# A two-layer graph attention kernel: float8 masks, a check on VectorE, all layer-two comparisons on ScalarE, and a last run closed in halves

## The reference

```python
def layer0(h):                                   # 4 heads of 32 features
    Wh = (h @ W).reshape(N, 4, 32)
    e = leaky_relu(s_src[:, None, :] + s_dst[None, :, :], 0.2)
    attention = softmax(where(adj[:, :, None] > 0, e, -9e15), axis=1)
    return elu(einsum('ijh,jhd->ihd', attention, Wh).reshape(N, 128))

def layer1(x):                                   # hyperbolic, one head of 128 features
    x_tan = arctanh(|x|) * x / |x|
    e = leaky_relu(x_tan @ a[:128] + (x_tan @ a[128:]).T, 0.2)
    attention = softmax(where(adj > 0, e, -9e15), axis=1)
    return proj(expmap0(attention @ x_tan))

x = layernorm(x + layer0(x))
x = layernorm(x + layer1(x))
```

## Time and profile before

| what | us |
|---|---|
| median of 3 runs (lowest 977.76, highest 983.52) | 979.15 |
| the profiled execution, its own time | 978.17 |
| span of that execution in the trace | 976.3 |
| PE busy in the span | 854.6 |
| DVE busy | 771.7 |
| ACT busy | 759.4 |

### The profile page before, as it was taken

The page is one execution under the profiler, slowest core; times in us unless marked ns, Lnnn a source line. Parts: engine busy times, 40 slices in busy tenths (PEclk is TensorE's granted clock), DMA queues, the critical chain, the costliest instruction groups (busy, mean ns, idle before and its releaser), DMA issues.

```text
span 976.3 us, 24788 instructions
## 1 busy us (share of the span) xinstructions
PE 854.6 (88%) x10868; PEld 698.6 (72%) x10868; DVE 771.7 (79%) x1415; ACT 759.4 (78%) x933; POOL 94.9 (10%) x177
## 2 busy tenths in 40 slices
PE   8468999989999899999999992999999999899940
PEld 6468999989999899999998951555555555455520
DVE  3857898899988999889977897986859594949316
ACT  3868988888999879999889865367877686868751
POOL 2200000000000000000000100003131222212210
PEclk9879999999999999999999997899999999999975
DMA  8988278704568045040300040209494949576750
GB/s 143 172 83 203 64 71 95 222 24 49 66 75 228 24 39 73 25 196 23 110 3 24 19 177 1 98 12 361 170 388 152 402 152 368 190 308 220 279 211 12
DMA packets 55731, 135.01 MB, mean 138 GB/s; under 512 B 7746, under 2 KB 32708, under 8 KB 54980
## 3 DMA queue, kind: packets, MB, share of 16 engines
q0 software_dynamic: 26240, 83.90, 36.8%
q1 hardware_dynamic: 29380, 49.50, 13.9%
HBM read 162.60 MB, written 21.12 MB: 188 GB/s over the span
## 4 chain that ended last, share of the span: by engine, by line
PE 42%; DVE 26%; DMA 13%; ACT 11%; issue 7%; SPq 0%; DVEq 0%; ACTq 0%
PE bank L613 32%; DMA ring<-in_adj_dram 5%; PE bank L985 4%; ACT masks L695 4%; DMA moving<-in_adj_dram 4%; DVE ring L561 4%; DMA s_rows<-score_rows 3%; DVE ring L580 3%; ACT ring L548 2%; PE bank L464 2%; ACT s_rows L750 2%; ACT masks L451 2%; DVE ring L590 1%; PE bank L972 1%; DVE ring L584 1%
## 5 line engine op out<-in xcount | busy, mean ns | idle before, releaser
L613 PE MATMUL bank<-moving,ring 128*128 128x99 bf16 (+1 forms) x6400 | 461.8, 220 | 10.7 <-DVE ring L590 7.6
L613 PEld LDWEIGHTS bank<-moving,ring 128*128 128x128 fp8e4 x6400 | 390.9, 98 | 15.2 <-DVE ring L590 8.6
L548 ACT ACTIVATE ring<-s_rows,scores 128x1024 fp8e4<-128x1024 f32 x356 | 377.5, 1142 | 15.6 <-PE bank L613 14.2
L613 PE MATMUL bank<-moving,masks 128*128 128x99 bf16 x1792 | 243.3, 210 | 26.5 <-DVE ring L580 15.6
L613 PEld LDWEIGHTS bank<-moving,masks 128*128 128x128 fp8e4 x1792 | 176.7, 99 | 28.3 <-DVE ring L580 16.5
L985 PE MATMUL bank<-moving,masks 128*128 128x387 bf16 x1152 | 195.6, 328 | 0.0
L985 PEld LDWEIGHTS bank<-moving,masks 128*128 128x128 fp8e4 x1152 | 112.7, 98 | 79.1
L580 DVE SCALAR_TENSOR_TENSOR ring<-ring,masks 128x1024 int32<-128x1024 int32 x89 | 108.3, 1217 | 4.7 <-ACT ring L548 4.6
L590 DVE TENSOR_TENSOR ring<-masks,ring 128x1024 int32<-128x1024 int32 x72 | 88.2, 1225 | 26.4 <-PE bank L613 24.6
L750 ACT ACTIVATE s_rows<-moving,minus_one 128x1024 fp8e4<-128x1024 int32 x76 | 86.9, 1144 | 26.9 <-DMA moving<-in_adj_dram 26.3
L561 DVE TENSOR_SCALAR ring<-s_rows,neg_d 128x1024 uint8<-128x1024 f32 x156 | 106.9, 750 | 0.0
(11 more groups left out here) (183 smaller groups left out, 750.6 us busy)
## 6 DMA issues: line engine op xcount, KB each, us to landing
moving<-in_adj_dram POOLq DMA_DIRECT2D x76, 512.0 KB, 6.6
ring<-in_adj_dram POOLq DMA_DIRECT2D x52, 512.0 KB, 6.3
masks_kept<-masks SPq DMA_DIRECT2D x4, 4096.0 KB, 18.4
masks<-masks_kept SPq DMA_DIRECT2D x8, 2048.0 KB, 23.7
adj_tiles<-in_adj_dram POOLq DMA_DIRECT2D x24, 512.0 KB, 8.4
s_rows<-score_rows SPq DMA_DIRECT2D x14, 512.0 KB, 5.7
adj_tiles<-in_adj_dram POOLq DMA_DIRECT2D x16, 256.0 KB, 15.1
feat<-in_x_dram SPq DMA_DIRECT2D x4, 512.0 KB, 5.7
```

The lines of the kernel that those rows point to most:

```text
L548: last = act.activation(j_tile(below, k), s_rows[:, h % 2, :], ACT.Sign, bias=scores[:, g * JU + k, h:h + 1], saturate=False)
L613: last = pe.matmul(bank[b][:, at + lo:at + hi], mask, moving[:, j, h, lo:hi], start=first, stop=(j == T - 1), skip_group_check=True)
```

## The change

- **Float8 cast.** The transfers that load `adj` convert int32 to float8 (1 becomes 0x38) where they converted to uint8. ACT's copies out of PSUM scale by 8/7 where they scaled by 64, so a 1 is 0x40 again.
- **OR check of kept masks.** The check reads the 16 MB of `masks_kept`, in 32 parts of 512 KB, by POOL's queue. It runs on DVE: each part is combined with `seen` by a bitwise OR of 128 x 1024 int32. There are two buffers for loads, so part k is loaded when part k - 2 has been combined. The parts stand in DVE's list behind the splits of iteration e = 2, 3, 4, 5 and behind the closing of e = 6, in batches of 6, 6, 7, 6 and 7. `raise_flag` folds `seen` by four ORs and one AND. ACT does no checks.
- **All layer-two comparisons on ScalarE.** `signs` does eight tiles of each group in every run, and `split_group` is one AND with shift and one XOR on 128 x 1024 int32.
- **Two pairs of side buffers** at the change of layers: groups 1 and 3 use one, group 2 the other. Steps of groups 1 and 2 and the first pieces of the closing are written in another order on DVE and ACT.
- **Last run closed in halves.** Run 7 is read, closed and stored in two halves of two tiles.

```diff
-        adj_tiles = sb("adj_tiles", [P, AHEAD, N], U8, fast)
+        adj_tiles = sb("adj_tiles", [P, AHEAD, N], FP8, fast)
...
-                           ACT.Copy, bias=BOTH_SIGNS, scale=float(TWO)).then_inc(turned_out, 1)
+                           ACT.Copy, bias=BOTH_SIGNS, scale=ONE_TO_TWO).then_inc(turned_out, 1)
...
-        check_in = [of_ring(CHECK).bitcast(I32) for _ in range(2)] + \
-            [moving_flat[:, free + n * 2 * CHECK:free + (n + 1) * 2 * CHECK].bitcast(I32) for n in range(3)]
+        seen, *check_in = [moving_flat[:, free + n * 2 * CHECK:free + (n + 1) * 2 * CHECK].bitcast(I32) for n in range(3)]
         CB = len(check_in)
...
-            for k in range(GT if e == 0 else HALF):
+            for k in range(GT):
                 j = g * GT + k
                 last = act.activation(j_tile1(sides_of_run[y][1], j), s_rows1[:, y, :], ACT.Sign,
...
-        def check_part(act, k):
-
-            act.wait_ge(check_loaded[k % CB], 16 * (k // CB + 1))
-            if k >= 4:
-                act.wait_ge(check_done, k - 3)
-            act.activation(check_out[k % 4], check_in[k % CB], ACT.Square, bias=minus_one[:, 0:1], scale=2.0,
-                           accum_out=checks[:, k:k + 1], saturate=False).then_inc(check_done, 1)
+        def check_part(dve, k):
+
+            dve.wait_ge(check_loaded[k % CB], 16 * (k // CB + 1))
+            dve.wait_ge(check_done, k + 1)
+            dve.tensor_tensor(seen, seen, check_in[k % CB], ALU.bitwise_or).then_inc(check_done, 1)
...
+            n = CHECK
+            while n > CHECK // 16:
+                n //= 2
+                step(dve.tensor_tensor(seen[:, 0:n], seen[:, 0:n], seen[:, n:2 * n], ALU.bitwise_or))
+            step(dve.tensor_tensor(seen[:, 0:n], seen[:, 0:n], low_bits, ALU.bitwise_and))
...
                     if k >= CB:
-                        pool.wait_ge(check_done, k - CB + 1)
-                    pool.dma_start(check_in[k % CB], adj_flat[:, k * CHECK:(k + 1) * CHECK]).then_inc(check_loaded[k % CB], 16)
+                        pool.wait_ge(check_done, k - CB + 2)
+                    if k == 0:
+                        pool.wait_ge(kept, 16 * NC)
+                    pool.dma_start(check_in[k % CB], kept_flat[k // (CHECKS // NC), :, (k % (CHECKS // NC)) * CHECK:
+                                                               (k % (CHECKS // NC) + 1) * CHECK]).then_inc(check_loaded[k % CB], 16)
...
                 act.wait_ge(moving1_ready, 2)
+                elu_exp(act, NC - 1)
+                round_part1(act, 1, 0)
+                round_part1(act, 2, 0)
+                round_part1(act, 1, 1)
                 signs(act, 0, 1)
-                round_part1(act, 1, 0)
-                round_part1(act, 1, 1)
-                elu_exp(act, NC - 1)
+                round_part1(act, 2, 1)
                 signs(act, 0, 2)
-                round_part1(act, 2, 0)
-                round_part1(act, 2, 1)
...
                 weigh_group(dve, 1)
+                weigh_group(dve, 2)
                 take_high1(dve, 1)
+                close_piece(NC - 1, 0)
                 take_middle1(dve, 1)
                 split_group(dve, 0, 1)
-                close_piece(NC - 1, 0)
-                weigh_group(dve, 2)
                 take_high1(dve, 2)
+                close_piece(NC - 1, 1)
                 take_middle1(dve, 2)
                 split_group(dve, 0, 2)
-                for n in range(1, 5):
+                for n in range(2, 5):
                     close_piece(NC - 1, n)
...
                         for g in range(NG):
                             split_group(dve, e + 2, g)
+                    if e == 0:
+                        begin_checks(dve)
+                    while done < CHECKS * max(e - 1, 0) // (NR - 3) and done < CHECKS:
+                        check_part(dve, done)
+                        done += 1
                     if e == NR - 2:
                         raise_flag(step)
+                for lo in (0, RT // 2):
+                    evacuate_run(dve, NR - 1, lo, lo + RT // 2)
+                    finish_run(step, NR - 1, lo, lo + RT // 2)
```

More of the change, by code:

```diff
@@ L20 @@
 BOTH_SIGNS = float(0x8080)
+ONE_TO_TWO = 8.0 / 7.0
 LARGEST_SCORE = (40.0, 75.0)
@@ L287, in __init__, with dve @@
                 self.stored = sems(f"{name}_stored0", f"{name}_stored1")
[L289 to L292, removed]
+                self.turns, self.answers, self.stores = 0, 0, [0, 0]
+            def dve(self, step, v, e, lo=0, hi=RT):
+                dve, y, tiles = step.engine, e % 2, hi - lo
+                raw2, raw, scratch, norm, gain, big, root = (self.small[:, k, lo:hi] for k in range(7))
+                work, result = self.work[:, lo:hi, :], self.result[:, y, lo:hi, :]
+                before = self.turns
+                self.turns += 3
                 step(dve.tensor_tensor(work, v, v, ALU.mult))
@@ L315, in dve @@
                 step(dve.tensor_tensor(gain, gain, scratch, ALU.mult))
-                step(dve.tensor_tensor(work, v, over(gain, RT, F), ALU.mult))
+                step(dve.tensor_tensor(work, v, over(gain, tiles, F), ALU.mult))
                 step.need(result_at)
                 step(dve.tensor_tensor(result, result, work, ALU.add))
-                for t in range(RT):
-                    last = dve.bn_stats(self.stats[:, t, 0:6], result[:, t, :])
+                for t in range(tiles):
+                    last = dve.bn_stats(self.stats[:, lo + t, 0:6], result[:, t, :])
@@ L321, in dve @@
                 step(last)
-                for t in range(RT):
-                    last = dve.bn_aggr(self.mean_var[:, t, :], self.stats[:, t, 0:6])
+                for t in range(tiles):
+                    last = dve.bn_aggr(self.mean_var[:, lo + t, :], self.stats[:, lo + t, 0:6])
                 step(last)
-                dve.tensor_scalar(raw2, self.mean_var[:, :, 1], LN_EPS, None, ALU.add).then_inc(self.asked, 1)
-                dve.wait_ge(self.given, e * 3 + 3)
+                dve.tensor_scalar(raw2, self.mean_var[:, lo:hi, 1], LN_EPS, None, ALU.add).then_inc(self.asked, 1)
@@ L327, in dve @@
+                dve.wait_ge(self.given, before + 3)
                 newton_root(step, root, raw2, scratch)
                 step(dve.reciprocal(root, root))
-                for t in range(RT):
-                    last = dve.tensor_scalar(result[:, t, :], result[:, t, :], self.mean_var[:, t, 0:1], root[:, t:t + 1],
+                for t in range(tiles):
+                    last = dve.tensor_scalar(result[:, t, :], result[:, t, :], self.mean_var[:, lo + t, 0:1], root[:, t:t + 1],
                                              ALU.subtract, ALU.mult)
@@ L332, in dve, with act @@
                 last.then_inc(self.ready, 1)
[L334 to L338, removed]
+            def act(self, act, lo=0, hi=RT):
+                raw2, raw, scratch, norm, gain, big, root = (self.small[:, k, lo:hi] for k in range(7))
+                for to, frm, func in ((raw, norm, ACT.Sqrt), (gain, scratch, ACT.Tanh), (root, raw2, ACT.Sqrt)):
+                    self.answers += 1
+                    act.wait_ge(self.asked, self.answers)
@@ L1075, in _ @@
                     signs(act, 1, g)
-                act.wait_ge(minus_ready, 1)
-                done = 0
-                for e in range(NR):
-                    fast_closing.act(act, e)
+                for e in range(NR - 1):
+                    fast_closing.act(act)
                     if e + 2 < NR:
@@ L1082, in _ @@
                             signs(act, e + 2, g)
-                    while done < min(CHECKS, CHECKS * (e + 1) // (NR - 1)):
-                        check_part(act, done)
-                        done += 1
+                fast_closing.act(act, 0, RT // 2)
+                fast_closing.act(act, RT // 2, RT)
             @block.vector
@@ L1203, in _ @@
                     split_group(dve, 1, g)
-                for e in range(NR):
+                done = 0
+                for e in range(NR - 1):
                     evacuate_run(dve, e)
```

117 lines of the change are left out of this document (54 added, 63 removed).

## The result

The changed kernel takes 1010.43 us (median, 1009.38 to 1017.1) against 980.96 us for the kernel before on the same chips: a ratio of 1.032 (95% interval 1.027 to 1.037), slower. The profiled execution took 1010.38 us with a span of 1008.6. The forecast was 1005.6, in a range of 982 to 1018. Predicted and measured stand 4.8 us apart.

The account below looks back on a forecast made before the run. DVE's loop (45.0 us against PE's 42.64) was the bound; with checks, iterations of 52.3, 56.8 and 52.3 us put the flag at 970.9; halves of 25.4 end at 996.3, plus 7.4 and 1.9 gives 1005.6 us, range 982 to 1018.

Parts of the forecast that it names:

- The loop of DVE and ACT: Layer two, one iteration without checks: 38.2 us where it was 45.0, fitting under PE's 42.64.
- The batches: Checks on DVE behind the last split, with reloads through two buffers: 14.1 us for six parts, 18.6 for seven.
- rival B: Check loads land as slowly as in company: 5.6 us gives 1022, 6.6 gives 1034; chance 0.08.
- The waits and gaps: Layer two: DVE waits about twelve times for check loads, some 3 us each; PE's last four gaps about 8 us or more.
- The clock after a gap: PE's first 16 matmuls after a 4.31 us gap took 4.33 instead of 2.84 us; 1.5 us added to run 7.
- The change of layers: New order of steps on DVE and ACT adds 3.8 us, so PE starts group 3 of run 0 at 615.9.
- The end: Behind PE's last matmul: two halves take 25.4 us where a whole took 18.2, hiding nothing; end at 996.3.
- The float8 cast: Loading adj in layer one: taken as 0; a conversion slower by a tenth would cost up to 8 us.
- A: Rival: check loads land while DVE waits elsewhere, a batch costs 7.5 or 8.75 us, total 966.2; chance 0.09.
- C: Rival: conversion to float8 is slower at the start, total 1006 to 1014 or more; chance 0.05.
- D: Rival: DVE's loop is shorter; 3 us less in five iterations gives 990; chance 0.10 with what lies between A and the forecast.

Follow-up runs that it names:

- run 7: Not an experiment: PE's last run of layer two, which the changed kernel reads, closes and stores in two halves; forecast to end at 971.3.
- run 3: Not an experiment: a run of PE in layer two, forecast to end at 757.9; no gap stood ahead of it in the changed kernel.
- run 2: Not an experiment: a run of PE in layer two, forecast to start at 672.6 and end at 715.2.
- best_old: The changed kernel with checks between the splits, six buffers for their loads and the old order at the change of layers: 944.34 us, 0.963 of the kernel before.
- best_u8: best_old with the uint8 conversion and the scale of 64 as in the kernel before: 944.54 us, 0.964 of the kernel before.
- run 0: Not an experiment: PE's first run of layer two, at the change of layers; forecast to end at 628.8, measured 3.2 us later than in the kernel before.

## Why the prediction was right, point by point

- **The loop of DVE and ACT.** Worked out as 38.2 us without checks; the trace has 37.8 (766.55 to 804.36, and the same in the next two iterations). It fits under PE's 42.64: no gap ahead of run 3, and none at all without checks.
- **The batches.** Right in kind, off in size where masks are loaded beside them. Forecast 14.1 us for six parts and 18.6 for seven. Measured, in the order of the iterations: 18.0, 17.2, 20.4, 14.0 and 17.7. The mis-sized term is the landing of 4.2 us, in the first three. The last two batches meet no load of masks, their landings have medians of 3.9 and 3.8 us, and they came out at 14.0 for 14.1 and 17.7 for 18.6. The first three stand beside SP's 2 MB of masks. In the first batch SP issued its masks at 756.11, POOL the next load at 757.75, and it took 7.64 us to land. No load of the check landed in under 3.7 us. The chain of waits of the changed kernel shows a load issued ahead of the masks and the one behind them:

```profile
751.37 4.83 DMA moving<-masks_kept
...
757.46 0.28 issue
757.75 7.64 DMA moving<-masks_kept
```

  The collision was named as what speaks for rival B, but priced nowhere in the forecast. The batches were forecast too short by 7.8 us in sum. Against this stand an iteration forecast too long by 0.4 us three times and a first batch that began 2.1 us before the forecast's 750.6, since run 2 started without the gap of 1.2 us that was worked out ahead of it. Together that is +4.5 us: the reading of the last banks began at 975.48, where the forecast had 970.9. That is the difference of the totals but for 0.2 us. That the total came within 4.8 us is in part luck, as errors of 3.3 us went the other way.
- **The waits and gaps.** The forecast said DVE would wait about twelve times, some 3 us each. It waited 22 times, 0.85 to 4.93 us, 48.0 us in sum: every part but the first two of a batch waited. The working had the second load of a pair land by the time the first part was combined. In each batch the first reload landed in 3.7 to 4.0 us; the second, issued 1.3 us behind it, took 4.6 to 5.0. The gaps of PE were 11.6, 9.7, 13.1 and 6.8 us, the last below the "about 8 us or more". PE ended at 977.4, not about 971.
- **The clock after a gap.** Taken as 1.5 us for a run from a gap of 4.31 us. After gaps of 7 to 13 us PE's first 16 matmuls took 4.75 to 5.35 instead of 2.84 us, so 1.9 to 2.5 us. It hardly mattered to the total, since DVE's loop set the pace.
- **The change of layers.** 3.8 us forecast; group 3 came 3.6 us later than before, 3.2 counted from the layer's first matmul, and the medians of two kernels that differ in this alone stand 4.5 us apart. Group 1 was forecast at 576.6 and came at 576.76.
- **The end.** Two halves of 12.7 us were forecast, 12.7 and 12.8 measured. That they would hide nothing was right for the changed kernel, and only there.
- **The float8 cast.** Taken as 0; best_old and best_u8 differ by 0.2 us, less than the range of either.
- **The rivals.** A (loads that don't count) is what six buffers give: 966.2 worked out, 963.92 measured. It wasn't what happened, because POOL can't ask for part k before part k - 2 is done. B happened in part, in the three batches that met SP's masks (3.9, 3.1 and 1.8 us over the forecast). C didn't happen, and of D only 0.4 us an iteration.

What the forecast did not say is that the checks need not stand on the loop at all: DVE's waits for ACT's signs, about 2.4 us ahead of each split, hold them.

## What to carry to other kernels

Work that has to be done somewhere should stand where its engine waits anyway, not behind the last step that another engine needs: the same 32 operations cost 62 us behind the splits and nothing between them. With two buffers only two parts were loaded ahead of a batch, and every further pair cost a round trip of issue and landing on the consumer's list; with six buffers no part waited. Closing the last run in halves gained 3.3 us where DVE was there 19 us before the last matmul ended, and lost 7.3 where it was there 1.9 us before, since it pays the small steps twice.

## What was not expected of the hardware

A 512 KB load that was issued 1.6 us behind a 2 MB load on another queue took 7.64 us to land, where such loads with no masks beside them took 3.8 and 3.9 us at the median of two batches. And the price of a gap in PE's work can't be told from its length here. It is the extra time of the first 16 matmuls behind it: nothing after gaps of up to 2.8 us, 1.5 us after one of 4.31 us (before), 2.5 us after one of 4.15 us (six buffers), 1.9 to 2.5 us after gaps of 7 to 13 us (the changed kernel), and 1.3 us after one of 11.3 us (last run whole).
